# Routed network in two halves: routing weights handed on by DRAM, and another order of the normalisation in gated attention

## The reference, cut to what matters

```
t = rmsnorm(x, ln2_w)
probs = softmax(t @ gate_w.T)
topv, topi = top_k(probs, 6);  topv = topv / sum(topv)
cw = zeros((T, 16)).at[token, topi].add(topv)
g = einsum('td,eid->eti', t, eg_w);  u = einsum('td,eid->eti', t, eu_w)
routed = einsum('eti,edi,te->td', silu(g) * u, ed_w, cw)
shared = silu(t @ sg_w.T) * (t @ su_w.T) @ sd_w.T
out = x + routed + shared
```

```
xn = rmsnorm(layernorm(x), norm_w)
attn = softmax(mask((xn @ wq.T) (ctx @ wk.T)^T / 4))
x = x + sigmoid(xn @ wg.T) * ((attn @ (ctx @ wv.T)) @ wo.T)
```

## Time and profile before

| | us |
|---|---|
| median of three runs (4550.22, 4557.97, 4559.98) | 4557.97 |
| the profiled execution's own time | 4553.52 |
| its span in the trace | 4551.8 |

### The profile page before, as it was taken

One profiled execution on the slowest core, in us unless ns is written; L12 is line 12 of the kernel. 1 busy time (PEld: TensorE's weight loads), 2 busy tenths in 40 slices (PEclk: granted clock), 3 DMA queues, 4 the chain that ended last, 5 costly groups with the idle time before them and its releaser, 6 DMA issues. The chain is left out here.

```text
span 4551.8 us, 76151 instructions
## 1 busy us (share of the span) xinstructions
PE 4012.4 (88%) x25840; PEld 3344.1 (73%) x25840; DVE 2689.9 (59%) x6149; ACT 2073.9 (46%) x5350; POOL 913.3 (20%) x746
## 2 busy tenths in 40 slices
PE   7885999999898877999999996999979998887791
PEld 4554899999776765888888885888868886665771
DVE  6877989989576336555555554433343334776633
ACT  6884666666223434444444443333333333665140
POOL 1112332333001431000000000222222222000245
PEclk9997999999998987999999998999989998998595
DMA  2001000000001014111111112000010000001344
GB/s 68 14 15 44 1 1 0 0 0 1 26 21 45 0 61 137 38 39 40 38 38 40 40 38 74 18 5 10 6 59 11 9 6 24 12 12 31 98 135 130
DMA packets 118894, 157.39 MB, mean 35 GB/s; under 512 B 15856, under 2 KB 83280, under 8 KB 118224
## 3 DMA queue, kind: packets, MB, share of 16 engines
q1 hardware_dynamic: 111744, 135.01, 9.4%
q0 software_dynamic: 6864, 18.75, 1.5%
HBM read 126.59 MB, written 27.13 MB: 34 GB/s over the span
## 5 line engine op out<-in xcount | busy, mean ns | idle before, releaser
L1213 ACT ACTIVATE peer_tab<-peer_sims 128x128 f32<-128x128 f32 x1024 | 305.6, 393 | 0.0
L1220 POOL TENSOR_TENSOR peer_tab<-peer_sims 128x2048 f32<-128x2048 f32 x64 | 246.2, 3867 | 289.4 <-ACT peer_sims L1197 260.2
L1268 DVE SCALAR_TENSOR_TENSOR peer_tab<-peer_tab,peer_th 128x2048 f32<-128x2048 f32 x128 | 298.2, 2370 | 2.6 <-ACT peer_tab L1213 2.3
L1285 PE MATMUL bank<-ident,peer_tab 128*128 128x128 f32 x2048 | 247.9, 275 | 24.6 <-DVE peer_tab L1268 24.6
L1285 PEld LDWEIGHTS bank<-ident,peer_tab 128*128 128x128 f32 x2048 | 234.5, 142 | 37.9 <-DVE peer_tab L1268 25.4
L1335 PE MATMUL bank<-peer_wd,peer_hh 128*128 128x256 f32 x1024 | 242.0, 379 | 1.2 <-DVE peer_hh L1326 1.2
L1308 PE MATMUL bank<-peer_hT,peer_wg 128*128 128x256 f32 x1024 | 242.7, 380 | 0.0
L645 DVE TENSOR_TENSOR moe2a_b<-moe2a_a,bank 128x512 f32<-128x512 f32 x104 | 71.4, 687 | 271.1 <-PE bank L551 239.6
L633 POOL TENSOR_TENSOR moe2a_hh_lo<-moe2a_hh,moe2a_hh_hi 128x512 fp32r<-128x512 f32 x104 | 141.0, 1356 | 369.9 <-ACT moe2a_hh_hi L624 353.0
L1308 PEld LDWEIGHTS bank<-peer_hT,peer_wg 128*128 128x128 f32 x1024 | 195.2, 191 | 26.6
L645 DVE TENSOR_TENSOR moe2b_b<-moe2b_a,bank 128x512 f32<-128x512 f32 x96 | 65.9, 687 | 250.1 <-PE bank L551 219.6
(11 more groups left out here) (538 smaller groups left out, 11453.1 us busy)
## 6 DMA issues: line engine op xcount, KB each, us to landing
mha_wo<-mha_wo SPq DMA_DIRECT2D x128, 256.0 KB, 2.7
m_y_rows<-moe_y SPq DMA_DIRECT2D x79, 128.0 KB, 1.7
att_ctxT<-in_ctxT_dram SPq DMA_DIRECT2D x32, 256.0 KB, 2.6
lin_ctxT<-in_ctxT_dram SPq DMA_DIRECT2D x16, 256.0 KB, 2.7
...
```

The source lines that it names most:

```text
L1213: i = nc.scalar.activation(tab[g][h][:, b * P:(b + 1) * P], sims[:, g, h, P:2 * P], ACT.Identity, bias=sims[:, g, h, b:b + 1])
L1220: nc.gpsimd.tensor_tensor(out=tab[g][h][:].rearrange("p (a b) -> p a b", b=P), in0=sims[:, g, h, P:2 * P].unsqueeze(1).broadcast_to([P, NB ...
L1268: nc.vector.scalar_tensor_tensor(out=tab[g][h][:], in0=tab[g][h][:], scalar=th[:, g, h:h + 1], in1=tab[g][h][:], op0=ALU.is_ge, op1=ALU.mu ...
L1285: i = nc.tensor.matmul(TB[n % 2][:, j * P:(j + 1) * P], tab[g][h][:, blk * P:(blk + 1) * P], core.ident[:], start=(j == 0 and h == 0), sto ...
```

## The change

`moe2a` stores each tile's finished `cwT` (all 128 rows, 256 KB) in a DRAM buffer of its own, and `moe2b` loads them from there and has no router: no gate weights, no logits, softmax, top 6, transposes, copies, nor `low_weights_dve`. In `moe2a` SyncE stores a tile's weights behind the load of the activations two tiles on, and `cwT_act` waits before it overwrites a stored buffer. In `moe2b` SyncE loads the first two tiles' weights behind all quads, and those of tile t behind its activations, when all CW matmuls of tile t - 2 are done; the first CW matmul of a tile waits for that load. Each half has four more semaphores. In gated attention `stats_dve` goes ahead of `result_dve`, `square_dve` behind it, both ahead of the second spread.

```diff
-def ffn_stage(core, name, kind, front_kind, blocks, top_k=0, first=0, store=False, inputs=None, inputs_loaded=False):
+def ffn_stage(core, name, kind, front_kind, blocks, top_k=0, first=0, store=False, inputs=None, inputs_loaded=False, shares_out=None, shares_in=None):
...
         sel_zeroed = sem("sel_zeroed")
+        shares_stored, shares_loaded = ([sem(f"shares_{n}{i}") for i in range(2)] for n in ("stored", "loaded"))
         router_chain = Chain(sem("router_chain"), 9)
-        NF = NTR + 2
+        NF = NTR + (2 if shares_in is None else 0)
     if relu:
...
             act.wait_ge(cwT_ready, t)
+        if shares_out is not None and some(t - 1):
+            act.wait_ge(shares_stored[par], (t // 2) * 16)
         nc.scalar.activation(cwT[0:32, par, :], F[0:32, :], ACT.Copy)
...
                 pe.wait_ge(hh_ready, n - 1)
-            if j == 0:
+            if j == 0 and shares_in is None:
                 pe.wait_ge(cwT_ready, t + 1)
+            if j == 0 and shares_in is not None:
+                pe.wait_ge(shares_loaded[par], (t // 2 + 1) * 16)
             if is_first(t) and j % QB == 0:
...
+    def store_shares_sp(sp, t, par):
+        sp.wait_ge(cwT_ready, t + 1)
+        sp.dma_start(shares_out[:, bass.ds(t * TILE, TILE)], cwT[:, par, :].bitcast(FP32)).then_inc(shares_stored[par], 16)
+
+    def load_shares_sp(sp, t, par):
+        if some(t - 1):
+            sp.wait_ge(cw_ready, (t - 1) * NB)
+        sp.dma_start(cwT[:, par, :].bitcast(FP32), shares_in[:, bass.ds(t * TILE, TILE)]).then_inc(shares_loaded[par], 16)
+
     def residual_dve(dve, t):
...
+    routed = gated and shares_in is None
+
     def front_pe(pe, t, j):
...
             transposes_pe(pe, t)
-        if gated and j == LOGITS:
+        if routed and j == LOGITS:
             logits_pe(pe, t)
-        if gated and j == WEIGHTS:
+        if routed and j == WEIGHTS:
             cwT_pe(pe, t)
...
                 loaded_act(act, t, par)
-        if gated and j == ROUTER:
+        if routed and j == ROUTER:
             router_act(act, t)
-        if gated and j == WEIGHTS:
+        if routed and j == WEIGHTS:
             cwT_act(act, t, par)
...
             norm_dve(dve, t)
-        if gated and j == ROUTER:
+        if routed and j == ROUTER:
             router_dve(dve, t)
         if split and j == LOW:
-            if gated:
+            if routed:
                 low_weights_dve(dve, t, par)
...
     if gated:
-        loads = [(gw[:], args[name[:4] + "_gate"].rearrange("(c p) e -> p c e", p=P))]
+        loads = [] if shares_in is not None else [(gw[:], args[name[:4] + "_gate"].rearrange("(c p) e -> p c e", p=P))]
         raws = [sb(f"raw{n}", [P, QB * P]) for n in range(2 * C)] + [sb("raw_wd", [P, QB, D]), sb("raw_sel", [P, QB * P])]
...
             if not ln:
-                with sp.Fori(2, NT) as t:
-                    load_front_sp(sp, t)
+                if shares_in is not None:
+                    load_shares_sp(sp, 0, 0)
+                    load_shares_sp(sp, 1, 1)
+                with sp.Fori(1, NT // 2) as pair:
+                    for par in range(2):
+                        load_front_sp(sp, pair * 2 + par)
+                        if shares_out is not None:
+                            store_shares_sp(sp, pair * 2 + (par - 2), par)
+                        if shares_in is not None:
+                            load_shares_sp(sp, pair * 2 + par, par)
+                if shares_out is not None:
+                    for par in range(2):
+                        store_shares_sp(sp, NT - 2 + par, par)
+                    for par in range(2):
+                        sp.wait_ge(shares_stored[par], 16 * NT // 2)
             if store:
...
                 split_act(act, 0, GATE_UP)
-                router_act(act, 0)
-                cwT_act(act, 0, 0)
+                if routed:
+                    router_act(act, 0)
+                    cwT_act(act, 0, 0)
                 split_act(act, 0, DOWN)
...
                 split_dve(dve, 0, GATE_UP)
-                router_dve(dve, 0)
-                low_weights_dve(dve, 0, 0)
+                if routed:
+                    router_dve(dve, 0)
+                    low_weights_dve(dve, 0, 0)
                 split_dve(dve, 0, DOWN)
...
                 spread_dve(dve, t + 1, nxt, KM_DVE[0:1])
+            if g == 1 and exists(t + 2):
+                stats_dve(dve, t + 2)
             if exists(t1):
                 result_dve(dve, t1, p1, g1)
+            if g == 1 and exists(t + 2):
+                square_dve(dve, t + 2)
             if g == 1 and exists(t + 1):
...
             if g == 1 and exists(t + 2):
-                stats_dve(dve, t + 2)
-                square_dve(dve, t + 2)
                 rows_dve(dve, t + 2)
...
             attention_inputs.close()
-            ffn_stage(core, "moe2a", "gated", "scratch", blocks=13, top_k=6)
-            ffn_stage(core, "moe2b", "gated", "scratch", blocks=12, top_k=6, first=13)
+            shares = nc.dram_tensor("moe2_shares", (P, T), FP32, kind="Internal").ap()
+            ffn_stage(core, "moe2a", "gated", "scratch", blocks=13, top_k=6, shares_out=shares)
+            ffn_stage(core, "moe2b", "gated", "scratch", blocks=12, top_k=6, first=13, shares_in=shares)
         if 6 in stages:
```

## The result

The changed kernel takes **4528.4 us**, median of 5 runs (4526.6 to 4534.7), against 4557.97 us before. The measured ratio is 0.9946 (95% interval 0.9936 to 0.9957), so 24.6 us are saved (19.6 to 29.2). The two medians themselves are 29.6 us apart; the ratio puts the kernel before near 4553, where its profiled execution (4553.5) and its medians on other chips (4550.9 to 4553.6) lie too. One more run of the kernel before, at 4812.04 us, fell in a slower state and is left out. The forecast was 4528, the range 4518 to 4540. The span of the profiled execution is 4526.4 us, 25.4 shorter than before; its granted clock is 0.939 over the whole span, 0.937 before.

What follows compares the result with a forecast made beforehand. It took TensorE's own instruction list and its few waits to bound the routed network's second half. Terms 25.0 + 2.4 - 0.6 + 1.6 = 28.4 us saved gave 4529.6 or 4525.1 by starting point; forecast 4528, range 4518 to 4540.

Steps and rivals of the forecast that it cites:

- 15.8 for logits and transposes: Second half: removing TensorE's logits (1.80) and transposes (0.45) saves 2.25 us for each of seven tiles, 15.8 us.
- 1.00 a tile for the table loads: Second half: two ScalarE table loads make `hh_lo` late; removing them saves 1.00 us a tile, 7.0 us, or 0.
- 0.27 a tile beside `hT_lo`: Second half: GpSimd's `hh_lo` stands still beside VectorE's `hT_lo`; an earlier `hT_lo` saves 0.27 a tile, 1.9 us, or 0.
- The start, 2.4: Second half's start: earlier first matmuls and weights against the wait for shares, gain 2.4 us, from 0 to 5.
- Semaphores, 0.6: Both halves: clearing four more semaphores each costs 0.3 us a stage, 0.6 us lost.
- Gated attention's start, 1.6: First units: scores at 3840.3, transposes 0.7 earlier, TensorE perhaps sooner at its upper clock; gain 1.6 us, bounds 0.5 and 2.6.
- Gated attention, steady, 0: Later units: TensorE's 2.10 us wait for the residual stays, units as long as before; gain 0.
- 1 (only the instructions go): Second half: the 0.75 wait and the 4.70 stay, the start gives nothing; 4542 us. Chance 7%.
- 2: Gated attention: the new order shortens every unit by 2.1 us, 27 us more saved; 4501 us. Chance 3%.
- 3: Gated attention: the second key spread comes too late, making the kernel slower than before. Chance 2%.
- 4: Second half: with its last gaps gone, TensorE is granted a clock under 1.00, eating up 28 us. Chance 1%.
- 5: Second half: change fails, for example each tile's shares hold TensorE 4.2 us, 34 us in all; 4563 us. Chance 2%.

Runs made afterwards that it cites:

- e5: Changed kernel with TensorE's eight logit matmuls and four transposes put back in the second half for tiles 1 to 7, results unread; 4541.4 us, ratio 0.9976.
- e6: Changed kernel with ScalarE's one router Exp put back in the second half for tiles 1 to 7, on constants, result unread; 4521.8 us, one run.
- e11: Changed kernel with VectorE's softmax and top 6 chain and ScalarE's Exp put back in the second half, on constants, results unread; 4526.0 us, one run.
- e10: Changed kernel with VectorE's 32x512 subtraction put back ahead of `hT_lo` in each tile of the second half, result unread; 4522.7 us, one run.
- e7: Changed kernel with `square_dve` directly behind `stats_dve`, ahead of the result, in gated attention; 4523.2 us, ratio 0.9925.
- e12: Changed kernel with VectorE's softmax and top 6 chain put back in the second half, on constants, with a Copy instead of the Exp; 4530.4 us, one run.
- e3: Changed kernel with the first two tiles' share loads issued behind the first group of weights' loads instead of the last; 4521.0 us, ratio 0.9934.
- e1: Kernel before with only gated attention's new VectorE order, router kept in both halves; 4551.1 us, ratio 0.9996.

## Why the prediction was right or wrong, point by point

- **What bounds the kernel**: right for this stage. The router's own instructions on TensorE, put back alone, bring 14.0 of the 23.3 us back (e5).
- **15.8 for logits and transposes**: right in size (seven times 1.80 and 0.45), but counted without what they had covered. The split of the third quad in the first tile was late by 0.22 us (the step of 4.65 behind the logits) before and is by 1.93 now. The prediction did not look at this step: it took all that the 91 blocks have over plain ones for removed. The 0.22 was what stuck out from under the logits. The difference, 1.7 us, is what the steady part came out short by (forecast 25.0, measured 23.3).
- **1.00 a tile for the table loads**: right size, wrong cause. The step that failed is "two table loads (for Exp and back to Silu) lie ahead of it, so `a`, VectorE's `hh` and GpSimd's `hh_lo` come late". Alone they make 0.39 (e6). VectorE's softmax, with the first table load inside it, ended last (e11). I followed the wait back to ScalarE because the table loads stood out, and did not compare with the row of `b`, which started 0.66 us after `a` was done. Since the change removes both, the sum did not suffer; an edit that had moved the Exp alone would have.
- **0.27 a tile beside `hT_lo`**: right in size and cause; 1.49 us against the forecast's "under 1.9", and 0.25 a tile when put back (e10). The Trainium skill's rule (SBUF — State Buffer, "SBUF: two separate sides"), by which a VectorE operation with two SBUF inputs and a GpSimd one that reads SBUF lock each other out for a whole instruction, agrees with e10 (2.30 us), e7 (1.86) and e12 (VectorE's 0.85) in both directions.
- **The start, 2.4**: measured 3.1. The chain came out within 1.1 us at each link, counted from GpSimd's memset: third quad's down weights issued after 18.3 us (forecast 19.4; 25.7 before), first selection matmul after 24.4 (24.8), second 4.66 later (4.9), third 4.42 later (4.4). The queue ahead of the shares was part of it: behind the third quad's last parts the first two loads of shares took 5.1 us to land, the six later ones, with only activations ahead of them, 2.7 (medians in after). By e3, issued earlier they are no longer waited for. Whether they could pass the weights in the queue no run tested.
- **Semaphores, 0.6**: not shown. GpSimd's idle time around the end of the first half, which clears its semaphores there, is 6.88 us against 6.75; but it is 6.85 in e1 with the old number, and 6.04 to 7.28 in the other kernels with the new one. A cost of 0.3 us a stage is below that spread.
- **Gated attention's start, 1.6**: wrong. Only 0.7 of it was worked out; the rest was put on the clock without a row. The wait for the rows went as forecast, and the scores start 3.0 us (e1) and 2.7 (after) later behind the first unit's transposes, where 2.6 were forecast. But TensorE's wait ahead of them grew by 1.3 and 2.1 us, and behind it its granted clock was 0.76 and 0.55 over the scores, not 1.00, so that they took 2.45 and 3.45 us, not 1.94. The step that failed is "done after their 1.94 at 3842.2, [...] so the transposes start 0.7 earlier": they came 0.1 us later in e1 and 0.8 in after, counted from the first unit's (18.0 and 18.7 against 17.9). The other half, the upper level sooner in what follows, is seen in after (0.84 against 0.73) and not in e1 (0.73). The 1.6 that before and after show side by side is within what traces of one order differ by.
- **Gated attention, steady, 0**: right as to the wait: the 2.10 us for the residual stand in twelve units of before, and 2.10 to 2.28 in as many of after and of e7. Single units differ by over 0.5 us between before and after, which the prediction named as a sign of being wrong; they differ as much between traces of one order, and the whole stage is 0.5 us shorter.
- **Rivals**: 1 (only the instructions go) is out by the profile after, which has neither the wait nor the 4.70; e11 and e10 name their causes. 2 and 3 are out by e1. 4: the granted clock in the second half stays 1.00. 5: no tile but the first waits for its shares.
- **The sum**: forecast 28.4 from terms of 25.0, 2.4, -0.6 and 1.6; by the traces it is 23.3 + 3.1 + 0 for the order, so 26.4; the spans differ by 25.4, the ratio gives 24.6. The forecast of 4528 was thus 28.4 below a start of 4556.4, near the median of before (4557.97), where the ratio puts the kernel at 4553: the start was some 3 us too high and the sum 2 to 4 too large, and the two errors cancel. That is luck, though of a size that the range allowed for.
